# The sums over repeated rows in a graph-network kernel as two float32r products in place of one fp32 product

## The reference

```
h    = x @ W_in2f
Wij  = (softplus(f_ij @ W_filt1 + b_filt1) - ln 2) @ W_filt2 + b_filt2
x_ij = h[dst] * (Wij * edge_weight[:, None])
agg  = segment_sum(x_ij, src, 6250)
out  = (softplus(agg @ W_out1 + b_out1) - ln 2) @ W_out2 + b_out2
y    = layernorm(x + out)
```

## Time and profile before

| | |
|---|---|
| median of 3 runs | 2372.86 us |
| the profiled execution | 2375.85 us, span 2373.8 us |
| mean granted TensorE clock | 0.967 of full speed |
| TensorE busy | 2162.8 us |
| VectorE busy | 1676.7 us |
| ScalarE busy | 1642.3 us |
| GpSimd busy | 1828.8 us |
| DMA | 250.03 MB, 105 GB/s on average |

### The profile page before, as it was taken

The page is one execution under the profiler, slowest core; times in us unless marked ns, Lnnn a source line. Parts: engine busy times, 40 slices in busy tenths (PEclk is TensorE's granted clock), DMA queues, the critical chain, the costliest instruction groups (busy, mean ns, idle before and its releaser), DMA issues.

```text
span 2373.8 us, 60910 instructions
## 1 busy us (share of the span) xinstructions
PE 2162.8 (91%) x16558; PEld 1441.8 (61%) x16558; DVE 1676.7 (71%) x3915; ACT 1642.3 (69%) x3676; POOL 1828.8 (77%) x1148
## 2 busy tenths in 40 slices
PE   2488999999999999999999999999999999999947
PEld 1355666666656666666666666666666666666536
DVE  5466777777777777777776777777676768777627
ACT  0277777777777777777776877777776867777513
POOL 2068888888888888888888888888888888888831
PEclk8599999999999999999999999999999999999979
DMA  6676666666656666666666666666666656666555
GB/s 207 265 151 95 97 95 91 100 99 90 97 95 94 97 96 97 93 94 99 93 95 94 100 90 100 95 96 92 96 97 89 101 94 98 91 97 99 58 122 164
DMA packets 370946, 250.03 MB, mean 105 GB/s; under 512 B 88787, under 2 KB 350142, under 8 KB 370314
## 3 DMA queue, kind: packets, MB, share of 16 engines
q0 software_dynamic: 160560, 73.14, 32.6%
q1 hardware_dynamic: 199482, 155.27, 27.2%
q10 hardware_dynamic: 10476, 16.77, 1.9%
HBM read 149.90 MB, written 95.13 MB: 103 GB/s over the span
## 4 chain that ended last, share of the span: by engine, by line
DMA 44%; POOL 18%; PE 17%; issue 16%; DVE 3%; ACT 1%; POOLq 0%; SPq 0%; DVEq 0%; ACTq 0%
DMA table<-total,index 41%; POOL table L729 18%; PE unit_psum L1859 4%; PE unit_psum L1878 3%; PE both_psum L1815 2%; PE total_psum L1828 2%; PE pre_psum L1802 2%; DMA src_g<-in_src 1%; DMA h_parts<-h_out 1%; PE both_psum L2086 1%; PE both_psum L1840 1%; PE both_psum L1811 1%; PE both_psum L2084 0%; PE total_psum L2108 0%; PE pre_psum L2094 0%
## 5 line engine op out<-in xcount | busy, mean ns | idle before, releaser
L729 POOL DMA_INDIRECT table<-total,index x1115 | 1801.1, 1615 | 445.1 <-issue 244.6
L1859 PE MATMUL unit_psum<-moving,route_hot 128*128 128x386 bf16 x3136 | 608.1, 331 | 40.3 <-ACT ring L909 34.6
L879 ACT ACTIVATE h_dst<-both_psum,cols 128x128 f32<-128x128 f32 x1564 | 448.8, 385 | 104.2 <-PE both_psum L1840 104.2
L1878 PE MATMUL unit_psum<-scat_hot,ring 64*128 64x448 bf16 x4704 | 478.7, 351 | 9.6 <-DVE scat_hot L1416 6.1
L1859 PEld LDWEIGHTS unit_psum<-moving,route_hot 128*128 128x128 bf16 x3136 | 295.8, 99 | 267.5 <-ACT ring L909 103.6
L909 ACT ACTIVATE ring<-unit_psum 128x386 bf16<-128x386 f32 x784 | 373.2, 508 | 120.5 <-PE unit_psum L1859 82.0
L1815 PEld LDWEIGHTS both_psum<-w_f,hidden 128*128 128x128 f32 x3128 | 418.0, 194 | 18.3
L1815 PE MATMUL both_psum<-w_f,hidden 128*128 128x128 f32 x3128 | 418.8, 277 | 0.0
L1878 PEld LDWEIGHTS unit_psum<-scat_hot,ring 64*128 64x128 bf16 x4704 | 216.0, 94 | 216.9 <-DVE acc_t L1432 7.4
L1828 PE MATMUL total_psum<-message,same 128*128 128x129 f32 x2232 | 310.1, 281 | 4.0 <-DVE message L1344 2.4
L843 ACT ACTIVATE soft<-pre_psum 128x1024 f32<-128x1024 f32 x196 | 201.8, 1030 | 160.9 <-PE pre_psum L1802 159.8
(11 more groups left out here) (116 smaller groups left out, 1635.6 us busy)
## 6 DMA issues: line engine op xcount, KB each, us to landing
dst_b<-dst SPq DMA_DIRECT2D x391, 128.0 KB
src_b<-src SPq DMA_DIRECT2D x279, 128.0 KB, 4.3
f_t<-in_f_t SPq DMA_DIRECT2D x98, 256.0 KB
table<-total,index POOLq DMA_INDIRECT x1115
table<-zeros ACTq DMA_DIRECT2D x20, 640.0 KB, 5.6
window<-h_parts SPq DMA_DIRECT2D x391, 32.0 KB
parts<-table SPq DMA_DIRECT2D x48, 256.0 KB, 4.0
h_parts<-h_out SPq DMA_DIRECT2D x12, 384.0 KB, 5.4
```

Source lines behind the costliest of these rows:

```text
L729: pool.indirect_dma_start(tables[table], bass.IndirectOffsetOnAxis(index[:, i, k:k + 1], 0), total[:, i, k, 0:DIM], None, compute_op=ALU.a ...
L879: last = act.activation(h_dst[:, b, d], source, ACT.Copy, scale=cols[:, g[1] // HALF % 2, weight:weight + 1])
L1859: last = pe.matmul(unit_psum[:, k % 2, 0:MOVING], route_hot[:, tile, k * P:(k + 1) * P], moving[:, tile, :], start=(tile == 0), stop=(tile ...
L1878: last = pe.matmul(unit_psum[:, strip, 0:BUCKET], ring[rows, r[1] % RING, slot_tile(m), part * DIM:(part + 1) * DIM], scat_hot[rows, r[1] ...
```

## The change

- `same` is float32r, and `message` (two buffers, 128 columns) stays fp32. New are `part_hi` (two buffers, 130 columns) and `part_lo` (two buffers, 128 columns), both float32r; each part is meant to hold 12 bits of a message.
- ScalarE's `split_part` copies `message` to `part_hi` and so rounds it. VectorE's `take_part` subtracts `part_hi` from `message`, to `part_lo`. The column of powers of two lies in `part_hi`, twice (ROW is 130, an even number).
- `sum_repeated` makes eight products in place of four: for each tile `same` with `part_hi` (130 columns), then `same` with `part_lo` (128 columns), added in PSUM. It waits for both parts. `multiply` waits for the parts of the group two before it to be made instead of for the sum of three before.
- The orders of ScalarE, VectorE and TensorE in `unit` and `rest` are new throughout; those of SyncE and GpSimd, and which groups are routed, are as before. Of the new orders two places are shown.

```diff
-ROW = DIM + 1
+ROW = DIM + 2
...
-        same = sb("same", [P, 3, TILES, P], F32)
-        message = sb("message", [P, 3, TILES, ROW], F32)
+        same = sb("same", [P, 3, TILES, P], F32R)
+
+        message = sb("message", [P, 2, TILES, DIM], F32)
+        part_hi = sb("part_hi", [P, 2, TILES, ROW], F32R)
+        part_lo = sb("part_lo", [P, 2, TILES, DIM], F32R)
...
+            def split_part(g, kind):
+
+                if not exists(g):
+                    return
+                b = g[1] % 2
+                act.wait_ge(message_done, through(g))
+                done_with(act, total_mm_done, g, kind, 2)
+                done_with(act, part_lo_done, g, kind, 2)
+                act.activation(part_hi[:, b, :, 0:DIM], message[:, b, :, :], ACT.Copy).then_inc(part_hi_done, 1)
...
                 if kind(g[1]):
-                    done_with(dve, total_mm_done, g, kind, 3)
-                    dest = message[:, g[1] % 3, :, 0:DIM]
+                    done_with(dve, part_hi_done, g, kind, 2)
+                    done_with(dve, part_lo_done, g, kind, 2)
+                    dest = message[:, g[1] % 2, :, :]
...
+            def take_part(g, kind):
+
+                if not exists(g):
+                    return
+                b = g[1] % 2
+                dve.wait_ge(part_hi_done, through(g, kind))
+                done_with(dve, total_mm_done, g, kind, 2)
+                dve.tensor_tensor(part_lo[:, b, :, :], message[:, b, :, :], part_hi[:, b, :, 0:DIM], ALU.subtract
+                                  ).then_inc(part_lo_done, 1)
...
-                b = g[1] % 3
-                pe.wait_ge(message_done, through(g))
+                b, i = g[1] % 3, g[1] % 2
+                pe.wait_ge(part_hi_done, through(g, kind))
+                pe.wait_ge(part_lo_done, through(g, kind))
                 pe.wait_ge(same_done, through(g, kind))
                 done_with(pe, total_done, g, kind)
                 for k in range(TILES):
                     d = slice(k % 2 * ROW, (k % 2 + 1) * ROW)
-                    last = pe.matmul(total_psum[:, k // 2, d], same[:, b, k, :], message[:, b, k, :],
-                                     start=True, stop=True)
+                    pe.matmul(total_psum[:, k // 2, d], same[:, b, k, :], part_hi[:, i, k, :], start=True, stop=False)
+                    d = slice(k % 2 * ROW, k % 2 * ROW + DIM)
+                    last = pe.matmul(total_psum[:, k // 2, d], same[:, b, k, :], part_lo[:, i, k, :],
+                                     start=False, stop=True)
                 last.then_inc(total_mm_done, 1)
...
                 def r(n): return (u[0], u[1] // UNIT * PER_UNIT + n)
+                mark_repeated(g(-2), plain)
                 compare_dst(g(2))
+                make_index(g(-2), plain)
+                compare_src(g(1), plain)
                 multiply(g(0), plain)
+                compare_dst(g(3))
+                finish_hidden(pair(1))
+                take_part(g(0), plain)
                 compare_src(g(2), plain)
...
                 second_layer(g(0))
-                route(m(-1), 4); route(m(-1), 5)
+                route(m(-1), 2); route(m(-1), 3)
                 gather(g(1))
+                second_layer(g(1))
+                route(m(-1), 4); route(m(-1), 5); route(m(-1), 6)
+                first_layer(pair(2))
                 sum_repeated(g(0), plain)
```

More of the change, by code:

```diff
@@ L947, in unit @@
                 copy_total(g(4), plain)
+                split_part(g(5), plain)
                 soften_abs(pair(4))
@@ L956, in unit @@
                 keep_slots(m(1), 4); keep_slots(m(1), 5)
+                split_part(g(7), plain)
                 soften_abs(pair(5))
@@ L980, in unit @@
                 split_mid(r(2))
+                split_part(g(11), plain)
                 weigh_h_dst(g(12), plain)
@@ L1000, in unit @@
                 copy_total(g(14), plain)
+                soften_abs(pair(9))
                 split_mid(r(3))
+                split_part(g(15), plain)
+                columns(g(24), plain)
                 soften_exp(pair(9))
@@ L1075, in step_general @@
+                split_part((0, 390), plain)
+                copy_total((0, 390), plain)
             def step_general(g):
@@ L1454, in unit @@
[L1454 to L1463 removed]
+                take_part(g(1), plain)
@@ new lines, in unit @@
+                slot_one_hot(m(1), 0); slot_one_hot(m(1), 1); slot_one_hot(m(1), 2)
+                add_slice(m(0), 0)
+                slot_one_hot(m(1), 3)
+                add_slice(m(0), 1)
+                compare_dst(g(4))
+                finish_hidden(pair(2))
+                mark_repeated(g(1), plain)
+                multiply(g(2), plain)
+                make_index(g(1), plain)
+                slot_one_hot(m(1), 4); slot_one_hot(m(1), 5)
+                compare_dst(g(5))
+                compare_src(g(4), plain)
@@ L1510, in unit @@
+                mark_repeated(g(7), plain)
+                slot_one_hot(m(3), 0)
+                make_index(g(7), plain)
+                slot_one_hot(m(3), 1)
+                finish_hidden(pair(5))
+                take_part(g(8), plain)
+                add_slice(m(2), 0); add_slice(m(2), 1)
+                multiply(g(9), plain)
+                compare_dst(g(11))
+                slot_one_hot(m(3), 2); slot_one_hot(m(3), 3)
+                mark_repeated(g(8), plain)
                 slot_one_hot(m(3), 4)
-                mark_repeated(g(8), plain)
@@ L1512, in unit @@
-                multiply(g(9), plain)
                 make_index(g(8), plain)
                 slot_one_hot(m(3), 5)
+                compare_dst(g(12))
+                take_part(g(9), plain)
                 compare_src(g(11), plain)
-                compare_dst(g(12))
+                multiply(g(10), plain)
                 compare_src(g(12), plain)
-                multiply(g(10), plain)
+                compare_dst(g(13))
+                finish_hidden(pair(6))
                 mark_repeated(g(9), plain)
```

386 lines of the change are left out of this document (205 added, 181 removed).

## The result

The changed kernel takes 2398.63 us (median of 8 runs, 2389.46 to 2405.82), the kernel before 2375.78 us in the same comparison (8 runs, 2367.43 to 2379.44). The ratio is 1.010, 95% interval 1.0084 to 1.0116. 2411 was forecast, and slower.

What follows compares the result with a forecast made beforehand. The prediction took GpSimd, issuing scatters without a pause, to bound the kernel. The profiled 2375.85 us + 36 for delayed scatters + 2.3 at the start = 2414.1, less 3.0 to the median: 2411 us, range 2397 to 2430.

Steps and rivals of the forecast that it cites:

- GpSimd is the bound, not TensorE: Scatter loop: GpSimd issues 1115 scatters without a pause, 2146 us; the other engines run up to four groups ahead.
- The relief of TensorE is worth nothing: Loop: cheaper sums win no time, since GpSimd's waits for an index after the first are only 11 us.
- eight float32r products in 0.80 us, 100 us saved: A group's sum on TensorE: 0.80 us at bf16's pace, 0.36 less than now, 100 us over 279 groups.
- Rival (d): Sum: a float32r product costs as much as an fp32 one and TensorE sets the pace, 2697 us; chance 0.03.
- The subtractions cost +36 us by holding up scatters: VectorE's 279 two-SBUF-input subtractions delay GpSimd's scatters by 0.129 us each: +36 us, bounds 24 and 65.
- rival (c): GpSimd starves: each of 36 waits for an index grows by 1.33 us, 48 us more, 2459 us; chance 0.07.
- Rival (e): Each subtraction stops GpSimd for its whole 0.684 us: 191 us in place of 36, 2566 us; chance 0.03.
- In the loop the longer path costs nothing: From message to sum 1.33 us longer, but up to four groups of 7.7 us stand ahead of GpSimd: 0 us.
- The orders cost nothing: New orders of ScalarE, VectorE and TensorE: no term of their own, though they shift old instructions against the scatters.
- rival (a): Faster by phase: new orders put most two-SBUF-input instructions behind scatter starts; 2347 us if 37 us of delay remain; chance 0.16.
- (b): No change: the 279 subtractions fall behind the scatter starts, the old instructions stay, 2366 to 2380 us; chance 0.14.
- Start +2.3 us: Before the loop, with no store yet, the longer path moves the first scatter from 128.34 to 130.6 us: +2.3 us.

Runs made afterwards that it cites:

- a_no_lo_product: Changed kernel without the sum's second product (part_lo still made and waited for, its 4 matmuls a group left out): 2377.33 us, ratio 1.0006 to the kernel before.
- b_one_f32r: Kernel before, in its own orders, with message and same as float32r and one product for each tile, no split: 2360.92 us, ratio 0.9925.
- a_widths: Changed kernel with a probe ahead of its loop: 12 matmuls each of float32r, fp32 and bf16 at several widths, each with a weight load: 2425.38 us, once.
- b_extra_sbuf: Kernel before with one more VectorE subtraction of 128x512 for each plain group, both inputs in SBUF, result unused: 2403.07 us, ratio 1.0128.
- b_extra_psum: The PSUM twin: kernel before with one more VectorE subtraction for each plain group, one input in PSUM, one in SBUF: 2389.70 us, ratio 1.0059.
- a_lo_one_input: Changed kernel with part_lo made by a VectorE copy with one SBUF input, in steps of 128 elements, instead of the subtraction: 2435.23 us, ratio 1.0255.
- b_same_by_tile: Kernel before with compare_src as four 128x128 VectorE instructions with a scalar column in place of one with two SBUF inputs: 2342.36 us, ratio 0.9864.

## Why the prediction was right, and where not

The time came out in the range (2397 to 2430), 12 us under the forecast, but that is in part luck: two errors offset each other. Over the profiled executions, 22.9 us apart, the forecast had 36 us of longer scatters, nothing of a dry GpSimd and 2.3 us of a later start. The row of L733 has 5.2 us of longer scatters, 17.5 of idle time, and the start 0.2.

- *GpSimd is the bound, not TensorE.* Right for the kernel before: its idle time is within 2 us of the lowest seen. For the changed kernel it holds for all but some 19 us (362.4 against 343.1), in which GpSimd waits for the others.
- *The relief of TensorE is worth nothing.* The result looks so, but for another reason than given: there was no relief. The term "eight float32r products in 0.80 us, 100 us saved" is wrong; the first sum takes 1.10 us for 1.16, and 8 matmuls a group stayed 8 of the same length. Nor is real relief worth nothing: a_no_lo_product gets 21 us by it, b_one_f32r 15. The bound of 11 us from GpSimd's waits for an index missed that a relief also moves VectorE's work against the scatters, and that it covers what the change adds. Rival (d) had a float32r product as dear as an fp32 one; it costs half of one.
- *The subtractions cost +36 us by holding up scatters.* The mechanism is shown: 1.682 us a scatter against 1.541 in the PSUM twin, and 32.5 us for the subtraction as a whole. But the size of the term is wrong in this kernel: 18.5 us are longer scatters, 0.066 us each, half of the 0.129 forecast, since 89 of the 279 subtractions are badly placed where 120 of the 279 extra ones were, at 0.118. 16 us are GpSimd run dry, which I had given to rival (c). Rival (e), 0.684 us for each, is out.
- *In the loop the longer path costs nothing.* This step failed. The store of four groups isn't full after a return of the loop; idle time grew by 17.5 us. It is the mechanism of rival (c), at a third of its 48 us.
- *The orders cost nothing.* This step failed too, with the other sign: -19 us, by scatters that take 23 us less and 3.5 us more of idle time. It is the mechanism of rival (a). With it the medians add up as 2375.8 - 19 + 32.5 + 9 = 2398, by the way the runs were cut, so the sum is no check of its own. The counts given in rival (a) for badly placed `moving` and `same`, 46 and 59, come to 55 and 86 by its own stretch (0.5 us before to 0.1 after), and `rest_r` to 36 in place of 27.
- *Start +2.3 us.* It was +0.2. I took `finish_hidden` of pair 1 to end as late as before, at 126.08; in ScalarE's new order the softplus comes earlier and it ends at 124.09 (122.87 plus 1.22), the subtraction at 124.69.
- Of the signs named, the median scatter (1.54), x1115, the length of `part_lo` (0.683 us) and ScalarE's shorter wait (62 us) held. The mean rose to 1.620, under the 1.645 that I had asked for and just over the 1.615 that would have spoken for (a) or (b); the gap rose to 0.325 us, the first scatter came at 128.53 instead of 130 to 131, the sum's matmuls didn't halve, and TensorE's share didn't fall.

## What to carry to other kernels

Find the engine whose gaps are no longer than its own issue, and then ask of each edit what it does to that engine's instructions, also where it runs on another engine: here 279 subtractions on an engine that was 71% busy cost 1.4% of the time, and in the kernel before four small instructions in place of one, with more busy time, gave 1.4% back. Ask also where the engine's store runs thin, here behind each return of the loop: there a longer path costs time that the averages don't show. Before trading one wide-type product for two cheap ones, measure the product's pitch at the width and with the weight load that it will have. And a new order of the same instructions is an edit with a price of its own: run it alone.

## What the runs showed of the hardware that I had not expected

- A float32r matmul with its own weight load goes every 0.11 to 0.12 us from 128 to 256 columns, and every 0.23 us with 512, at the higher clock; bf16 every 0.056 us with 128 and every 0.22 with 512 (a_widths).
- A scatter that a VectorE instruction covers for over 0.4 us takes 1.682 us when that one has two SBUF inputs and 1.541 when one of the two is in PSUM (b_extra_sbuf, b_extra_psum); 1.751 with one SBUF input in 512-byte steps (a_lo_one_input). A 128x128 comparison of uint16 with a scalar column does not hold it up (1.556 for 1.560, b_same_by_tile).
- TensorE stands 3.7 us at a return of the loop in the changed kernel and 2.5 in the kernel before; its clock is at the lower level for the next 3.4 to 6.8 us, at all 13 returns in the one and at 7 in the other.
